# Order of one step in a fused attention kernel: queries, projection, residual sum and softmax moved

## What is computed

```
qh = split(layernorm(x) @ wq + bq);  kh, vh = split(ctx @ wk + bk), split(ctx @ wv + bv)
logits = einsum('bhqd,bhkd->bhqk', qh, kh) / sqrt(16) + mask * -1e9
attn = softmax(logits, axis=-1)
x = x + (einsum('bhqk,bhkd->bhqd', attn, vh) merged) @ wo + bo
```

## Time and profile before

| | |
|---|---|
| runs | 904.71 us median of 3 (903.69 to 904.86) |
| the profiled execution | 899.36 us, its span 897.6 us |
| PE busy | 807.6 us, 90% |
| DVE busy | 731.0 us, 81% |
| ACT busy | 601.3 us, 67% |
| POOL busy | 591.0 us, 66% |
| tile steps of attention 0 | 50.75 to 246.6 us |
| tile steps of attention 1 | 519.85 to 725.1 us |

### The profile page before, as it was taken

One profiled execution on the slowest core, in us unless ns is written; L12 is line 12 of the kernel. 1 busy time (PEld: TensorE's weight loads), 2 busy tenths in 40 slices (PEclk: granted clock), 3 DMA queues, 4 the chain that ended last, 5 costly groups with the idle time before them and its releaser, 6 DMA issues. The chain is left out here.

```text
span 897.6 us, 24372 instructions
## 1 busy us (share of the span) xinstructions
PE 807.6 (90%) x9237; PEld 660.1 (74%) x9252; DVE 731.0 (81%) x1597; ACT 601.3 (67%) x1106; POOL 591.0 (66%) x731
## 2 busy tenths in 40 slices
PE   5699999999799998799997799999998879999996
PEld 4587878788678887699996587778777645555564
DVE  3788888888677876488875788988889769999996
ACT  2366777776555541588871367777667779999995
POOL 2354778766326566077774988699988878777551
PEclk9799999999999999899999699999999999999997
DMA  8564599800002222466644865100303020004000
GB/s 274 74 261 176 202 386 391 351 3 2 2 26 94 86 98 100 113 212 203 217 165 153 279 96 76 21 3 2 49 3 49 2 36 24 30 24 89 25 30 30
DMA packets 55634, 100.04 MB, mean 111 GB/s; under 512 B 10208, under 2 KB 36448, under 8 KB 55520
## 3 DMA queue, kind: packets, MB, share of 16 engines
q1 hardware_dynamic: 38672, 70.12, 23.2%
q0 software_dynamic: 15232, 27.80, 12.2%
q10 hardware_dynamic: 1616, 0.58, 0.3%
HBM read 35.04 MB, written 59.24 MB: 105 GB/s over the span
## 5 line engine op out<-in xcount | busy, mean ns | idle before, releaser
L579 POOL TENSOR_TENSOR sm_a<-sm_a,mx_a 128x616 f32<-128x616 f32 x128 | 158.4, 1237 | 97.2 <-DVE mx_a L973 95.8
L875 ACT ACTIVATE pr_a<-sm_a 128x616 f32<-128x616 f32 x128 | 91.5, 715 | 88.6 <-POOL sm_a L579 88.6
L1267 POOL DMA_INDIRECT mixed<-rep,qidx_f x80 | 78.0, 975 | 47.7 <-DVE rep L1777 24.8
L748 PE MATMUL pT_a<-ident,pr_a 128*128 128x128 f32 x640 | 96.4, 281 | 7.4 <-ACT pr_a L875 5.4
L973 DVE TENSOR_REDUCE mx_a<-sm_a 128x8 f32<-128x616 f32 x128 | 99.0, 773 | 0.0
L771 PE MATMUL pO_a<-aw,ot_a 128*128 128x256 f32 x256 | 72.4, 405 | 20.9 <-DVE ot_a L994 20.2
L748 PEld LDWEIGHTS pT_a<-ident,pr_a 128*128 128x128 f32 x640 | 71.3, 142 | 21.9 <-issue 14.1
L1261 POOL DMA_INDIRECT slots<-sx,idx_f x48 | 47.8, 995 | 47.8 <-DVE idx_f L1664 34.7
L722 PE MATMUL pA_a<-sx,aw 128*128 128x128 f32 x512 | 72.4, 287 | 0.5 <-ACT sx L869 0.5
L771 PEld LDWEIGHTS pO_a<-aw,ot_a 128*128 128x128 f32 x256 | 43.3, 189 | 40.0 <-DVE ot_a L994 36.7
L722 PEld LDWEIGHTS pA_a<-sx,aw 128*128 128x128 f32 x512 | 66.5, 203 | 1.4 <-ACT sx L869 1.1
(11 more groups left out here) (354 smaller groups left out, 2526.7 us busy)
## 6 DMA issues: line engine op xcount, KB each, us to landing
slots<-sx SPq DMA_DIRECT2D x16, 2176.0 KB, 9.3
sx<-slots SPq DMA_DIRECT2D x40, 272.0 KB
x<-x_in SPq DMA_DIRECT2D x4, 1024.0 KB, 11.1
x<-mixed POOLq DMA_DIRECT2D x4, 1024.0 KB, 10.0
out_x<-x SPq DMA_DIRECT2D x32, 128.0 KB, 1.7
rep<-gu_in SPq DMA_DIRECT2D x10, 256.0 KB, 4.7
aw<-aw_in SPq DMA_DIRECT2D x2, 1024.0 KB, 7.0
ha<-mixed SPq DMA_DIRECT2D x2, 1024.0 KB, 7.2
```

The lines of the kernel that those rows point to most:

```text
L579: pool.tensor_tensor(heads, heads, mx[u][:, g, :].rearrange("p (h a) -> p h a", a=1).broadcast_to([P, HG, SK]), ALU.subtract).then_inc(shi ...
L748: mm = pe.transpose(pT[:, (J * t + j) % 2, (n % 4) * P:(n % 4 + 1) * P], pr[u][:, g, c * P:(c + 1) * P], sb["ident"][:])
L875: act.activation(pr[u][:, g, 0:NS], sm[u][:, g, :], ACT.Exp).then_inc(exped, 1)
L1267: pool.indirect_dma_start(dram["mixed"][:], bass.IndirectOffsetOnAxis(qidx[:, at:at + 1], 0), ys[q % 2][:, j, :], None).then_inc(out_moved ...
```

## The change

- **Queries** are made a step earlier, for tile t + 3, behind the weighing of tile t (before: for t + 2, behind the first transposes). They go to 128 free columns each of score banks 0 and 1 (`asked`), wait for the mask of tile t + 2 and are brought out by ACT in two pieces (before: by DVE in one).
- **The projection** of tile t - 2 goes to the left half of pA, and stands among the transposes (before: tile t - 1, into pO, in front of the scores). It waits also for `added` of the tile before. `weigh` waits for `o_norm` of the tile before, no longer for `added`.
- **The residual sum**, its statistics and their gathering are those of tile t - 2 and follow each other. There is one more step behind the last (`lay_out_steps(step, 4, 2)` on PE and DVE).
- **Softmax** goes once per tile: mask, maximum, shift and exponential of all 1232 columns. The maximum stands behind its mask in the same step.
- On ACT the work aside (weights of layer 0, norm of layer 1) moves ahead of the last `pt_out`.

Buffers:

```
-        sm = pair("sm", [P, G, NS])
-        mx = pair("mx", [P, G, HG])
+        sm = pair("sm", [P, ROWS_OF_HEADS * G * QS])
+        mx = pair("mx", [P, HEADS])
...
+        asked = lambda g: pS[:, g, G * QS:G * QS + P]
```

PE:

```
             def queries(t, u):
                 pe.wait_ge(xt_sb, t + 1)
-                count(pe, q_sb, t)
+                count(pe, masked, t)
...
-                        mm = pe.matmul(pA[:, D + g * P:D + (g + 1) * P], aw[:, k, g * P:(g + 1) * P],
+                        mm = pe.matmul(asked(g), aw[:, k, g * P:(g + 1) * P],
...
             def weigh(t, u):
-                count(pe, added, t)
+                count(pe, o_norm, t)
...
             def project(t, u):
                 pe.wait_ge(o_norm, t + 1)
+                count(pe, added, t)
                 for k in range(G):
-                    mm = pe.matmul(pO[:, 0:D], ot[u][:, k * P:(k + 1) * P], aw[:, k, 3 * D:4 * D],
+                    mm = pe.matmul(pA[:, 0:D], ot[u][:, k * P:(k + 1) * P], aw[:, k, 3 * D:4 * D],
...
                     turn_p(t, u, 0)
                     turn_p(t, u, 1)
-                if has(2):
-                    queries(t + 2, u)
+                if has(-2):
+                    project(t - 2, u)
                 if has(3):
                     turn_x(t + 3, 1 - u)
...
-                if has(-1):
-                    project(t - 1, 1 - u)
...
                 if layer == 1 and t == TOTAL:
-                    pe.wait_ge(q_sb, t + 3)
+                    pe.wait_ge(o_norm, t)
                     total()
                 if has(2):
                     scores(t + 2, u)
                 if has(0):
                     weigh(t, u)
+                if has(3):
+                    queries(t + 3, 1 - u)
...
-            lay_out_steps(step, 4, 1)
+            lay_out_steps(step, 4, 2)
```

ACT:

```
+            def q_out(t, u):
+                act.wait_ge(q_ps, t + 1)
+                count(act, scored, t - 1)
+                for g in range(G):
+                    last = act.activation(q[u][:, g * P:(g + 1) * P], asked(g), ACT.Identity,
+                                          bias=bqkv[:, 0, g:g + 1])
+                last.then_inc(q_sb, 1)
+
+            def exp(t, u):
+                act.wait_ge(shifted, t + 1)
+                count(act, pt_ps, J * (t - 1))
+                act.activation(pr[u][:, :, 0:NS].rearrange("p g (b n) -> p g b n", b=ROWS_OF_HEADS),
+                               sm[u][:].rearrange("p (b g n) -> p g b n", b=ROWS_OF_HEADS, g=G), ACT.Exp).then_inc(exped, 1)
```

DVE:

```
+                dve.tensor_tensor(sm[u][:].rearrange("p (b h k) -> p b h k", b=ROWS_OF_HEADS, k=SK),
+                                  pS[:, :, 0:G * QS].rearrange("p b (h k) -> p b h k", k=SK),
+                                  every.broadcast_to([P, ROWS_OF_HEADS, G * HQ, SK]),
...
-                dve.tensor_tensor(X[:, t, :], pO[:, 0:D], X[:, t, :], ALU.add).then_inc(added, 1)
+                dve.tensor_tensor(X[:, t, :], pA[:, 0:D], X[:, t, :], ALU.add).then_inc(added, 1)
...
                 if has(-1):
                     refine(t - 1, 1 - u)
                     normalise(t - 1, 1 - u)
-                if has(2):
-                    q_out(t + 2, u)
-                if has(1):
-                    largest(t + 1, 1 - u, 1)
+                if layer == 1 and t == TOTAL:
+                    scales()
+                if layer == 0 or t >= 0:
+                    aside(t)
+                if has(-2):
+                    add(t - 2)
+                    stats(t - 2, u)
+                    gather(t - 2, u)
...
+                if has(2):
+                    mask(t + 2, u)
+                    largest(t + 2, u)
```

127 lines of the change are left out of this document (48 added, 79 removed).

## The result

The changed kernel takes 887.9 us median (887.82 to 891.36, 4 runs), the kernel before 904.2 beside it: ratio 0.9837, 95% interval 0.9809 to 0.9865. So 16.3 us are gained by the medians, 14.7 by the ratio (12.2 to 17.3), and I had forecast 32.4. The time lies in my range, but the gain is half of the forecast. The profiled execution of the changed kernel took 891.36 us (span 889.6), the slowest of its four, that of before 899.36, its fastest; execution against execution the gain is 8.0 us.

The account below looks back on a forecast made before the run. The kernel was taken as bound by a loop through all engines and, almost equally, VectorE's 5.90 us of work. Window savings of 32.4 us off 904.71 gave 872 us; own case 866 to 880, range 859 to 890.

Parts of the forecast that it names:

- the sum: Both attention layers: savings of the windows between residual sums, together 32.4 us, taken off the 904.71 us median: 872 us.
- late steps of layer 1: Layer 1, VectorE scaling and clipping weights beside GpSimd's wide subtraction: 6.1 us gained less 0 to 6.3 held; 2.0 taken.
- The loop is cut: Attention steps: weighing waits only for normalise; 4.57 us of loop remain, under every other sum, so this wait goes to nothing.
- no effect: Rival, attention steps: VectorE's work sets the 6.43 us and wide operations return the gain; within 2 us of 904.7; chance 0.04.
- slower, ScalarE blocked: Rival, attention steps: exponential waits for the whole shift and holds ScalarE's later work; 6.7 us a step, 917 us; chance 0.05.
- TensorE's sum, 5.75, plain step 5.8: Attention steps: TensorE's work sums to 5.48 to 5.81 us, 5.75 taken; with VectorE's turns a step takes 5.8.
- my rival of that name: TensorE alone sets the pace in attention: 5.65 us a step, nothing held in late steps, 861 us; chance 0.16.
- VectorE's sum, 5.7: Attention steps: VectorE's work per step after the change is 5.7 us, or 5.15 without the early statistics.
- Take turns at nearly the same pace: Attention steps: TensorE and VectorE alternate, 1.4 us before the mask against 1.2 of transposes and scores; 5.8 us a step.
- The eviction of queries, 0.28: ScalarE in attention steps: each of two new evictions of 128 columns takes 0.28 us, between half of 0.376 and 0.376.
- The extra step has only projection, `add` and statistics: 0: End of each attention layer: the added step holds only what the last step holds now, so it costs 0 us.
- a rival, steps of 6.15 us: Attention steps stay at 6.15 us because evictions wedge before the transposes' or `add` comes late; 887 us; chance 0.23.

Follow-up runs that it names:

- e14: Changed kernel with zeros written evenly and the b2 transfer two steps earlier, queries brought out by VectorE in one operation instead of ScalarE: 876.5 us, ratio 0.9686.
- e5: Changed kernel with the zeros written evenly, 24 smaller transfers, one behind each residual sum, no longer waiting for the split of weights: ratio 0.9773.
- e3: Changed kernel with layer 1's scaling and clipping of weights moved on VectorE from behind normalise to ahead of the mask: 883.18 us, ratio 0.9782.
- e17: Changed kernel with zeros written evenly, b2 transfer two steps earlier, and weights scaled and clipped ahead of the mask: 872.59 us, ratio 0.9653.
- e6: Changed kernel with GpSimd's last transfer of attention 1 (bias b2 added into x) two steps earlier: ratio 0.9803.
- e7: Changed kernel with 30 unused 128x128 matmuls on TensorE behind its last work of attention 1: ratio 0.9867.
- e1: Changed kernel with the zeros written in 22 pieces of 1.6 MB instead of 16 of 2.2 MB: 882.41 us, ratio 0.9755.

## Why the prediction was wrong in size

The step that failed is the sum. It took what each window of `add` would save and carried it over to the whole time, with nothing for what lies around the windows: the extra step at the start, the transfers of zeros beside the faster steps, and the change to the feed-forward block. The transfers cost 9.6 us and the feed-forward block 6.4 in the profiled execution, the two layers' other terms 6.3. Inside the windows it mis-sized the late steps of layer 1, a gain of 2.0 that came out as a loss of 1.3. The mechanism itself, the loop cut by the moved projection, is as foreseen.

- **The loop is cut: right.** The projection waits for nothing, the weighing follows the scores. The rivals "no effect" and "slower, ScalarE blocked" fall with it.
- **TensorE's sum, 5.75, plain step 5.8: nearly.** It is 5.88, without a gap and in steps with and without early statistics, so TensorE alone sets it, as my rival of that name had it, only at 5.88 and not 5.65. From start to start in the step shown, forecast in brackets: transposes 0.88 (0.83), queries 0.99 (0.89), projection 0.86 (0.73), the last four transposes 0.53 (0.42), scores 0.74 (0.74), weighing 1.88 (1.87). The upper end of my sum, 5.81, was the nearer one. 0.08 in 27 steps of layer 0 are 2.2 us.
- **VectorE's sum, 5.7: right** by e14 (6.02 with an eviction of 0.34 more). "Take turns at nearly the same pace" was not needed; it has 0.45 us of idle a step in the second half of layer 0.
- **The eviction of queries, 0.28: wrong, 0.365**, about the 0.376 of twice the columns, so nearly all of it is fixed. No effect, ScalarE being covered.
- **"The extra step has only projection, `add` and statistics: 0": wrong.** My windows began at the first `add`, and `add` itself comes a step later: 6.7 us more from the first mask to it in layer 0, 6.35 in layer 1. The draining gives back part: 11.27 us for three intervals instead of 15.0. Over layer 0 the forecast was 18.5 us, and without stops it would be 13.5; over layer 1 to its last sum 13.9, measured 12.6. These two differences, 5.0 and 1.3, are 6.3 us of the gap; they hold the plain step above and the late steps below as well.
- **The edge I left out: the transfers, 9.6 us in the profiled execution.** The earlier trace rows showed DMA engines at 0.91 and I read that row for its engines alone. None of my rivals had it. e5 shows it.
- **Late steps of layer 1, gain 2.0: wrong, a loss of 1.3.** Seven late steps take 49.4 us (651.96 to 701.36), before 48.1 (664.85 to 712.98). I had the size of a hold, 0.9 us, exactly (1.638 less 0.736), and then took only two thirds of it as lost; all eight operations but one were held, one of them for 2.61 us in all. Here the Trainium skill was the better guide: "SBUF — State Buffer", "SBUF: two separate sides", has the loser of the shared ports blocked for the whole instruction, and by it I had written a gain of nothing. The trace agrees: the shift from 670.68 ends at 672.93, and the clip that it holds at 673.48. It adds what I left out: behind the held operation the mask is late, and TensorE with it. e3 and e17 show it, 4.7 and 3.7 us by the medians, 2.9 in both traces.
- **The feed-forward block, not in the sum at all: in the profiled execution 2.5 us of later start and 3.9 in the block, of which the slower clock explains about 2 in the mean of all profiles.** Shown by the traces of e6 and e7. I had looked at the attention layers only, since the change touches nothing else.

From the forecast: 32.4 less 6.3, 9.6 and 6.4 leaves 10.1 us, against 8.0 between the profiled executions; the rest is elsewhere, mainly in the expert phase. Against the medians' 16.3 this account takes off 6.2 us too much: the profiled execution of the changed kernel was 3.5 us above its median, that of before 4.8 below. The runs that take the two collisions out agree better: 24.4 and the 6.3 make 30.7 of the 32.4. How the 8.1 us of the collisions split between stops and change of phase in an ordinary execution stays open. That the time fell into my range is luck: it lies outside the 866 to 880 us of my own case, and inside the whole only because that reached to 890 for a rival, steps of 6.15 us, that did not happen.

## What to carry to other kernels

When a step gets shorter, list what is paced by it: a queue of transfers that by my estimate just fitted into 6.4 us no longer fits into 5.9, and work that lies behind a fixed latency (a transfer to land, a change of phase) comes into the open. Cut windows at something that the change does not move; a marker that moves a step hides a step. Where the Trainium skill and a median of a mixed row disagree about contention, ask which overlap the new order makes the rule, and price its followers too.

## What was not expected of the hardware

- TensorE stopped for 2.1 to 3.0 us in the middle of a group of matmuls with nothing to wait for, in stretches with the DMA engines at 0.93 to 1.02; in 60 us of e5 at 0.86 never. In the first four steps at 0.97, and in the kernel before at 0.98, with loads and writes as well, it hardly stopped.
- A change of phase waits for the landing of a transfer that GpSimd issued, 7.8 us behind its issue, though no instruction of that phase waits for it (VectorE waits for it later, in the feed-forward block): with the transfer two steps earlier GpSimd's idle is 1.83 us instead of 4.73.
- After 4.04 us of idle TensorE's clock was granted at 0.87 over 25 us, after 0.90 and 0.59 us at 1.00: about 2 us in a block of 171. Behind the stop of 2.96 us in layer 0 it was at 0.59 for 4.18 us, behind those of 2.11 and, in e1, 2.69 us at 1.00.
- Splitting one 1232-column subtraction on GpSimd in two (2.39 us for both, from 2.25) freed VectorE's clips but not three of four scalings, and gained nothing: part of the hold moved from one engine to the other.
